# Small reciprocals before the broadcast, squares and text context on GpSimd, exponentials ahead of the stages, and a later context load in a cross-attention and mixture-of-experts kernel

## The reference

```python
x = x + xattn(layernorm(x), ctx)          # x: 8 x 112 x 512, ctx: 8 x 375 x 512, 16 heads of 32
x = x + moe(layernorm(x))                 # 8 experts, the best 2 of each token
# xattn: ctx_img = ctx[:, :257], ctx_txt = ctx[:, 257:]
q     = rms_norm(linear(x, q_w, q_b), norm_q_w)
k     = rms_norm(linear(ctx_txt, k_w, k_b), norm_k_w);          v     = linear(ctx_txt, v_w, v_b)
k_img = rms_norm(linear(ctx_img, k_img_w, k_img_b), norm_k_img_w); v_img = linear(ctx_img, v_img_w, v_img_b)
out   = linear(attention(q, k, v) + attention(q, k_img, v_img), o_w, o_b)
# rms_norm: y * rsqrt(mean(y*y) + eps), so every projection is squared and summed over its 512 channels
# attention: softmax(q k / sqrt(32)) v, so every head has two sums of exponentials, one over image and one over text keys
```

## Time and profile before

| | us |
|---|---|
| three runs: median (lowest to highest) | 931.02 (930.43 to 933.33) |
| the profiled execution | 931.23 |
| its span from first to last instruction | 929.4 |
| TensorE matmul busy | 773.7 (83%) |
| VectorE busy | 588.3 (63%) |
| ScalarE busy | 505.8 (54%) |
| GpSimd busy | 69.6 (7%) |
| reciprocals L761, 32 of them | 55.7, mean 1741 ns |

### The profile page before, as it was taken

One profiled execution on the slowest core, in us unless ns is written; L12 is line 12 of the kernel. 1 busy time (PEld: TensorE's weight loads), 2 busy tenths in 40 slices (PEclk: granted clock), 3 DMA queues, 4 the chain that ended last, 5 costly groups with the idle time before them and its releaser, 6 DMA issues.

```text
span 929.4 us, 17429 instructions
## 1 busy us (share of the span) xinstructions
PE 773.7 (83%) x6238; PEld 676.3 (73%) x6238; DVE 588.3 (63%) x1001; ACT 505.8 (54%) x1154; POOL 69.6 (7%) x94
## 2 busy tenths in 40 slices
PE   2888989898989898773079999999999999999930
PEld 2566666666666666552079999999999999999920
DVE  5466767676767676746136767676767676767634
ACT  4566767676767676751044545454545555555510
POOL 2100000000000000000600000000000000000014
PEclk9989999999999999855579999999999999999975
DMA  7850102010202000407625656565656565656568
GB/s 245 312 210 1 64 11 64 12 64 11 63 12 65 11 22 11 158 11 260 204 86 187 233 184 236 185 235 183 236 184 236 184 236 184 234 183 237 181 226 259
DMA packets 33982, 137.53 MB, mean 148 GB/s; under 512 B 3712, under 2 KB 3728, under 8 KB 22928
## 3 DMA queue, kind: packets, MB, share of 16 engines
q1 hardware_dynamic: 31200, 129.23, 40.0%
q0 software_dynamic: 2736, 7.69, 2.9%
HBM read 115.36 MB, written 21.54 MB: 147 GB/s over the span
## 4 chain that ended last, share of the span: by engine, by line
PE 68%; DVE 9%; ACT 9%; issue 7%; DMA 3%; POOL 2%; SPq 0%; POOLq 0%; ACTq 0%; DVEq 0%
PE tiles L960 7%; PE tiles L962 7%; PE tiles L961 7%; PE scores L1191 4%; PE scores L1193 4%; PE scores L1192 4%; PE ptb L1051 3%; PE pvb L962 3%; PE pvb L961 3%; PE pvb L960 3%; PE ptb L962 3%; PE ptb L961 3%; PE ptb L960 3%; PE scores L1042 2%; ACT scr L543 2%
## 5 line engine op out<-in xcount | busy, mean ns | idle before, releaser
L776 DVE TENSOR_TENSOR w<-scr,w 128x2048 fp32r<-128x2048 f32 x76 | 174.2, 2292 | 84.6 <-ACT w L568 84.6
L568 ACT ACTIVATE w<-scr 128x2048 fp32r<-128x2048 f32 x76 | 144.8, 1907 | 63.2 <-PE scores L1193 59.3
L960 PE MATMUL tiles<-c,w 128*128 128x256 f32 (+1 forms) x272 | 83.0, 305 | 22.1 <-DVE c L672 17.5
L1051 PE MATMUL ptb<-ident,scr 112*128 112x112 f32 x384 | 64.4, 279 | 25.9 <-ACT scr L553 25.9
L960 PE MATMUL tiles<-w 128*128 128x256 f32 x288 | 81.5, 283 | 0.0
L961 PE MATMUL tiles<-w 128*128 128x256 f32 x288 | 81.5, 283 | 0.0
L962 PE MATMUL tiles<-w 128*128 128x256 f32 x288 | 81.5, 283 | 0.0
L961 PE MATMUL tiles<-c,w 128*128 128x256 f32 (+1 forms) x272 | 79.9, 294 | 0.0
L962 PE MATMUL tiles<-c,w 128*128 128x256 f32 (+1 forms) x272 | 79.9, 294 | 0.0
L1051 PEld LDWEIGHTS ptb<-ident,scr 112*128 112x128 f32 x384 | 44.1, 149 | 48.9 <-ACT scr L545 35.1
L553 ACT ACTIVATE scr<-ptb 128x336 f32<-128x336 f32 x128 | 59.9, 468 | 26.9 <-PE ptb L1051 26.9
(11 more groups left out here) (212 smaller groups left out, 2120.9 us busy)
## 6 DMA issues: line engine op xcount, KB each, us to landing
scr<-in_dram SPq DMA_DIRECT2D x86, 1024.0 KB, 4.8
slots_d<-xr SPq DMA_DIRECT2D x3, 2048.0 KB, 17.5
scr<-in_dram SPq DMA_DIRECT2D x8, 750.0 KB, 4.9
scr<-slots_d SPq DMA_DIRECT2D x10, 512.0 KB, 4.6
slots_d<-scr SPq DMA_DIRECT2D x9, 512.0 KB, 3.8
xn<-in_dram SPq DMA_DIRECT2D x10, 256.0 KB, 4.7
xb<-in_dram SPq DMA_DIRECT2D x8, 224.0 KB, 4.9
xr<-in_dram SPq DMA_DIRECT2D x8, 224.0 KB, 2.5
```

Of the source, the lines that this page charges most:

```text
L568: act.activation(EH[slot], raw[slot], ACT.Copy).then_inc(S["eh_done"], 1)
L776: dve.tensor_tensor(EL[slot], raw[slot], EH[slot].bitcast(F32), ALU.subtract).then_inc(S["el_done"], 1)
L960: pe.matmul(out, wh, xh, start=start, stop=False)
L1051: mm = pe.transpose(ptb[:, t * L:(t + 1) * L], probs[0:L, h % 4, t * P:(t + 1) * P], ident[0:L, 0:L])
```

## The change

- `invert_sums`: the eight sums are inverted into a small tile `rsum` (112 x 8); VectorE waits for that on a semaphore `inverted`, and copies it 32 times into `rx`.
- The six squares of a body go from ScalarE to GpSimd (`square`, a product of `kn` or `qn` with itself), in the order k0, [second layer norm's power], k1, k2, q, kx, k3.
- The high part of the text context goes from ScalarE (h = 2) to GpSimd, between the first layer norm's power and k0's square; its low part on VectorE moves from h = 3 to h = 6. Image part and text part get semaphores of their own. In body -1 both stay as they were.
- ScalarE at h = 0, 4, 8, 12 runs `weigh` ahead of the stages.
- SP loads the next context behind the store of x1 (in body -1 behind the load of x).

```diff
+            def next_context(b):
+                sp.wait_ge(S["ch0_done"], b + 2)
+                sp.wait_ge(S["ch1_done"], b + 2)
+                sp.wait_ge(S["cl_done"], 2 * (b + 2))
+                sp.dma_start(cr, ctxT[b + 2]).then_inc(S["c_in"], 16)
...
                     if b < LAST - 1:
-                        sp.wait_ge(S["ch_done"], 2 * (b + 2))
-                        sp.wait_ge(S["cl_done"], 2 * (b + 2))
-                        sp.dma_start(cr, ctxT[b + 2]).then_inc(S["c_in"], 16)
                         sp.wait_ge(S["xn_done"], b + 2)
                         sp.dma_start(xb[0:L, :], x[b + 2]).then_inc(S["x_in"], 16)
+                    if b < FIRST:
+                        next_context(b)
...
                     sp.dma_start(x1_d[b - 1], x1[0:L, :]).then_inc(S["x1_stored"], 16)
+                if FIRST <= b < LAST - 1:
+                    next_context(b)
+                if has_tail(b):
...
+            def square(name, b, p):
+
+                taken(pool, name, b)
+                if name == "q":
+                    to, of = sq[:, :, 0:L], qn[:, 1 - p, :, :]
+                elif name == "kx":
+                    to, of = sq[:, :, L + IMG:TOK], kn[1 - p][:, :, IMG:KEYS]
+                else:
+                    c = int(name[1])
+                    to, of = sq[:, c, L:L + IMG], kn[1 - p][:, c, 0:IMG]
+                pool.tensor_tensor(to, of, of, ALU.mult).then_inc(S["squares"], 1)
+
             def body(b, p):
                 if has_prep(b):
                     rstd(b + 2, mv1, ve1, rs1, "ln1")
+                    if not fixed(b, -1):
+                        pool.wait_ge(S["c_in"], 16 * (b + 2))
+                        taken(pool, "v2", b)
+                        pool.tensor_copy(c_part(cH)[1], cr[:, :, PARTS[1]]).then_inc(S["ch1_done"], 1)
+                    if not fixed(b, -1):
+                        pool.wait_ge(tile_ready[tile_use("ms", b - 1)[0]], tile_use("ms", b - 1)[1] + 1)
+                    square("k0", b, p)
                 if has_tail(b):
                     rstd(b, mv2, ve2, rs2, "ln2")
                 if has_prep(b):
+                    for name in ("k1", "k2", "q", "kx", "k3"):
+                        square(name, b, p)
...
-                if name == "q":
-
-                    taken(act, "q", b)
-                    act.activation(sq[:, :, 0:L], qn[:, 1 - p, :, :], ACT.Square).then_inc(S["squares"], 1)
...
-                    act.activation(sq[:, c, L:L + IMG], tiles[:, bank, 0:IMG], ACT.Square, bias=bias).then_inc(S["squares"], 1)
...
-                if name == "kx":
-                    taken(act, "kx", b)
-                    act.activation(sq[:, :, L + IMG:TOK], kn[1 - p][:, :, IMG:KEYS], ACT.Square).then_inc(S["squares"], 1)
...
+                    if h % 4 == 0 and has_heads(b):
+                        weigh(b, p, h)
                     for name in STAGE_AT[h]:
                         if has(name, b):
                             stage(name, b, p)
-                    if h % 4 == 0 and has_heads(b):
-                        weigh(b, p, h)
-                    if h == 2 and has_prep(b) and not fixed(b, -1):
-                        split_ctx(act, b + 2, 1)
...
-                dve.reciprocal(rx[0:L], sums[0:L, g % 2, :, :].unsqueeze(3).to_broadcast([L, 2, 4, HD])).then_inc(S["rsum_done"], 1)
+                dve.reciprocal(rsum[0:L], sums[0:L, g % 2, :, :]).then_inc(S["inverted"], 1)
+                dve.wait_ge(S["inverted"], NC * b + g + 1)
+                dve.tensor_copy(rx[0:L], rsum[0:L].unsqueeze(3).to_broadcast([L, 2, 4, HD])).then_inc(S["rsum_done"], 1)
...
-                    if h in (1, 3) and has_prep(b) and not fixed(b, -1):
-                        split_ctx_low(b + 2, h // 2)
+                    if h in (1, 6) and has_prep(b) and not fixed(b, -1):
+                        split_ctx_low(b + 2, h // 5)
```

More of the change, by code:

```diff
@@ L135, in cross_attention_moe @@
         vx = sb("vx", [P, 2, D])
-        rx = sb("rx", [P, 2, 4, HD])
+        rsum, rx = sb("rsum", [P, 2, 4]), sb("rx", [P, 2, 4, HD])
         rbc, pvn, af = sb("rbc", [P, 2 * L]), sb("pvn", [P, 2 * L]), sb("af", [P, L])
@@ L238, in cross_attention_moe @@
             "vbias_done", "nq_done", "vlast_mm", "vlast_sb", "vlast_out",
-            "x_in", "c_in", "ch_done", "cl_done", "xr_in", "xr_ob", "ln1_stats", "ln1_mv", "ln1_var", "ln1_rstd", "xn_done",
+            "x_in", "c_in", "ch0_done", "ch1_done", "cl_done", "xr_in", "xr_ob", "ln1_stats", "ln1_mv", "ln1_var", "ln1_rstd", "xn_done",
             "ln2_stats", "ln2_mv", "ln2_var", "ln2_rstd", "xh_done",
             "squares", "sum_a", "sum_b", "r_done", "rms_done", "q_done", "k_done", "qh_done", "ql_done", "kh_done", "kl_done", "rows_stored", "rows_in",
-            "s_ready", "max_done", "exp_done", "rsum_done", "t_ready", "pt_done",
+            "s_ready", "max_done", "exp_done", "inverted", "rsum_done", "t_ready", "pt_done",
             "pv_ready", "rb_done", "pv_read", "a_done", "cleared", "ah_done", "al_done", "x1_stored",
@@ L279, in split_ctx @@
             act.wait_ge(S["c_in"], 16 * n)
-            act.activation(c_part(cH)[i], cr[:, :, PARTS[i]], ACT.Copy).then_inc(S["ch_done"], 1)
+            act.activation(c_part(cH)[i], cr[:, :, PARTS[i]], ACT.Copy).then_inc(S[("ch0_done", "ch1_done")[i]], 1)
         @block.sync
@@ L670, in split_ctx_low @@
             def split_ctx_low(n, i):
-                dve.wait_ge(S["ch_done"], 2 * n - 1 + i)
+                dve.wait_ge(S[("ch0_done", "ch1_done")[i]], n)
                 dve.tensor_tensor(c_part(cL)[i], cr[:, :, PARTS[i]], c_part(cH)[i].bitcast(F32), ALU.subtract).then_inc(S["cl_done"], 1)
```

## The result

The changed kernel takes 919.44 us in the median of four runs (918.5 to 922.8) against 931.18 for the kernel before (930.43 to 933.33): a ratio of 0.9877 with a 95% interval of 0.9846 to 0.9907, that is 11.7 us or 1.2% less. The forecast was 923.0, with a range from 916 to 932. The profiled execution took 922.8, the longest of its four; a second profile of the same kernel took 917.89.

A forecast was written before the change was run, and what follows sets the result against it. A body was taken as TensorE's work plus its short waits, mostly caused by ScalarE. Gains of 2.72 us against losses of 1.0 and 0.3 made -1.42 a steady body, -8.0 with the other bodies: 923.0 us, range 916 to 932.

The forecast's parts named there:

- (1): k0's wait for the image context's low part, behind VectorE's long reciprocal, ends with the small reciprocal and copy: 0.49 us gained.
- (2): The second scores' wait for head 3's exponential ends, as Square and context copy leave ScalarE: 0.78 us a body gained.
- (3): Head 4's transposes no longer wait for a ScalarE copy, with `weigh` run first: 0.49 us a body gained.
- (4): Head 8's transposes no longer wait, with `weigh` first and one k2 copy gone from ScalarE: 0.96 us gained.
- kx and k3 on GpSimd: At the fourth scores, these squares make VectorE's sums and maxima 1.35 us late; the body loses 1.0.
- collision at h = 3: GpSimd's context copy and k0's square meet VectorE's two-input L772; it slips in between them, losing 0.3 us a body.
- rival A: VectorE isn't held up by GpSimd: a steady body gains 2.27 us, 917 in all; chance 0.14.
- rival B: GpSimd wins at h = 3 and L772 waits for copy and square: -0.72 a body, 927.5 us; chance 0.12.
- if L833 starts while k3's square runs, the blocking is wrong: Sign at VectorE's sum: starting before GpSimd's k3 square ends would show VectorE isn't held, so A holds.
- Rival D: Slower: kx and k3 squares on GpSimd cost twice the price, 3.8 us the pair; 938 us, chance 0.12.
- since it asks first: At h = 3, VectorE's L772 slips in between GpSimd's copy and k0's square: 0.3 us lost, 1.0 if waiting for both.
- Rival C: ScalarE's exponentials come first but only wait for something else, so (3) and (4) stay: 932 us, chance 0.12.

The follow-up runs named there:

- the second experiment: The kernel before with only the exponentials put ahead of the stages at every fourth head: 923.63 us, ratio 0.9909.
- them and both edits: The changed kernel with k0's square later on GpSimd and the squares of kx and k3 back on ScalarE: 909.94 us, ratio 0.976.

## Why the prediction was right, and where its terms were off

**The four waits.** All four went. Their sizes by the stretches and the single edits:

| term | forecast | measured |
|---|---|---|
| (1) k0's wait, reciprocal | -0.49 | -0.71 (reciprocal alone) |
| (2) second scores | -0.78 | -0.70 (-1.41 of the first stretch, less (1)) |
| (3) transposes of head 4 | -0.49 | -0.52 (exponentials alone) |
| (4) transposes of head 8 | -0.96 | -1.03 (third stretch) |
| kx and k3 on GpSimd | +1.00 | +0.57 (fourth stretch; gone with both on ScalarE) |
| collision at h = 3 | +0.30 | +0.57 (gone with k0's square later) |
| a steady body | -1.42 | -1.87 (11.22 over six) |

The measured terms make -1.82. The rest lies in the second stretch: 9.81 with k0's square later, 9.88 with the exponentials first alone; which part of the change gives it, no run isolates. All four waits that were to go went, and both losses came. The sum was 0.45 a body too cautious, and six bodies make 2.7 of the 3.6 us between 923.0 and 919.4.

The time alone is weak evidence for this. 919.44 lies at the very edge of the forecast's own 919.5 to 926.5 and is nearer to rival A's 917 than to 923.0. It came so near in part by luck: the collision at h = 3 went the way of rival B (0.27 more than forecast), and the squares of kx and k3 hid that (0.43 less than forecast, mostly because they are shorter than priced). Only the rows and the single edits tell the forecast from A. (The range is said to begin at "A's 916"; A's own sum is 917.)

**Term (1), sized too small.** The profile's 0.49 counts from the modelled end of a matmul, and for (2) to (4) the prediction added 0.15 for that. For (1) it did not. In the changed kernel k0 starts 0.18 after the start of the two transposes ahead of it, and 0.89 before: a wait of 0.71 hidden behind a row of 0.48 or 0.49. The copy and the small reciprocal cost what was assumed, 0.52 from the start of the first to the end of the second:

```profile
143.13 0.20 DVE L780 RECIPROCAL rsum<-sums 112x8 f32<-112x8 f32 x1
143.36 0.29 DVE L782 COPY rx<-rsum 112x256 f32<-112x256 f32 x1
```

**Term (2)** is what the second scores win by two edits together. Undoing one of them gives back 0.34 (text context on ScalarE) or 0.19 (squares on ScalarE) in the first stretch.

**Term (4) needs both edits.** With the exponentials first alone the third stretch wins 0.68. The remaining 0.35 comes only with the squares off ScalarE, as the two kernels with them there (0.68, 0.68) and the two without (1.03, 1.06) show. TensorE's starts tell where it goes: with the squares on ScalarE kt's first matmul comes 0.2 later, and the transposes of head 8 come another 0.15 later behind kt's, both too short for a row of waits. Of this stretch's squares only k2's stands ahead of both in ScalarE's order; no run moves it by itself.

**The squares, priced too high.** Groups by line and form in the changed kernel:

```profile
L452 POOL TENSOR_TENSOR scr<-scr 128x257 f32<-128x257 f32 x32 | 20.0, 624 | 58.6 <-ACT scr L535 58.6
L452 POOL TENSOR_TENSOR scr<-scr 128x472 f32<-128x472 f32 x8 | 7.8, 973 | 43.2 <-DVE scr L757 43.2
L452 POOL TENSOR_TENSOR scr<-qn 128x448 f32<-128x448 f32 x8 | 7.5, 937 | 3.1 <-DVE qn L752 3.0
```

0.62, 0.97 and 0.94 instead of 0.73, 1.18 and 1.13; the pair kx and k3 takes 1.55 in a row, not 1.91. L448, from which the price was taken, reads two different tensors; a square reads the same one twice. Whether that is the cause, no run isolates.

**The chain at the fourth scores.** Body 2 of the changed kernel, against the earlier trace rows:

```profile
169.97 0.64 DVE L757 TENSOR_TENSOR scr<-tiles,vec 128x472 f32<-128x472 f32 x1
...
170.69 1.55 POOL L452 TENSOR_TENSOR scr<-scr 128x472 f32<-128x472 f32 x2 [5.62 <-DVE scr L757]
...
171.70 1.06 DVE L854 TENSOR_TENSOR scr<-scr 128x487 f32<-128x487 f32 x1 [1.09 <-POOL scr L452]
...
173.96 0.68 DVE L772 TENSOR_REDUCE nmax<-scores 112x2 f32<-112x514 f32 x1
```

L854 starts when kx's square is done and lasts 1.06 instead of 0.67: it ends 0.52 after GpSimd's last square (172.24). Here the prediction's own sign misleads: "if L833 starts while k3's square runs, the blocking is wrong". Its successor L854 does start, at 171.70, while that square runs. The recorded start does not show that its data flow; the length does, 1.06 against 0.67 beside ScalarE's squares (the run with kx and k3 on ScalarE). From kx's bias to the maxima it is 3.99 instead of 3.16, +0.83 where +1.35 was forecast; 0.36 of the difference is the shorter pair. TensorE's ms waits 0.3 and the body loses 0.57. Rival D needed 3.1 us for the pair and is out.

**VectorE waits for GpSimd.** This was the step that no row showed. Timeline of body 2 at h = 3, against the earlier trace rows:

```profile
149.21 0.58 POOL L460 CAST c<-scr 128x472 fp32r<-128x472 f32 x1
149.29 0.78 PE L1063 MATMUL scores<-kq 32*112 32x376 f32 x12
149.55 0.94 DVE L793 TENSOR_TENSOR a<-af,a 128x112 fp32r<-128x112 f32 x1 [1.19 <-ACT a L584]
149.75 0.62 POOL L452 TENSOR_TENSOR scr<-scr 128x257 f32<-128x257 f32 x1
...
150.42 0.53 DVE L701 TENSOR_SCALAR xn<-xb,mv,rs 112x512 f32<-112x512 f32 x1
```

L793 (L772 before) was 0.28 and is 0.93 to 0.95 in all six steady bodies. It starts while the context copy runs, and ends 0.12 after k0's square, which started later than it: asking first did not help it, the next GpSimd instruction went ahead. The step of the forecast that failed here is "since it asks first". Rival B had it right, but its price of 1.0 was too high: copy and square are each some 0.1 shorter than priced, L793 is 0.66 longer than before, and the body loses 0.57. Moving the square took L793 back to 0.36. So each engine is seen waiting for the other, and rival A (917) is out, though the shorter squares brought the time to within 3 us of it. The Trainium skill (SBUF — State Buffer, "Who interferes with whom") says that the one that issues first holds the shared ports for its whole instruction. The traces agree for single instructions (L854's 1.06 beside k3's square; L793's 0.44 behind k0's square and L440's 1.05 beside L691, both in body 2 of the run with the text context on ScalarE). For two GpSimd instructions in a row, the context copy and k0's square, they add that VectorE, waiting since the first, also waits for the second.

**Rival C** (the exponentials only wait for something else) fell with the second experiment: 1.2 us a body from the order alone.

**SP, right for the wrong reason.** The prediction gave SP's part 0 and held it for unrelated. The whole change agrees with 0, but undoing it costs 29.5 us. The step that failed is "nothing is won", though the number 0 came out, by luck: the store's slack was looked at with the low part at h = 3, while the change puts that wait of SP three steps later. That this is the cause, the run with the low part back at h = 3 and the old order shows: 44.40 a body, as with the new order (44.38). The list of what stands behind the wait was made for the new order only.

**Bodies -1 and 0.** Body -1: +1.0 forecast, +0.99 in the second profile (48.20 against 47.21), with full clock at its end in both. The mechanism is seen too: TensorE's wait for the sums goes from 0.68 to 1.63, and with kx and k3 squared by ScalarE the first scores came at 47.06. Body 0: -0.5 forecast, -2.0 and -2.6 measured. The profile of before had two stretches of half clock in body 0 and the second profile of after none, so part of this is the clock; how much, these profiles don't tell.

## What to carry to other kernels

When the bound engine's waits are short and many, the order on the engine that feeds it can be worth more than the work taken off it: here the exponentials first (1.2 us a body) against all squares moved (a loss of 0.5). In this kernel work moved to an idle GpSimd was free only where VectorE had no instruction with two SBUF inputs at that time and nobody waited for the result. The four early squares were worth having (43.42 with them and both edits, 44.05 with all squares on ScalarE), the two late ones and the early place of k0's were not, and putting these right made 909.9 of 919.4. A wait that is moved in one engine's program moves everything queued behind it: check each order against each other change, not only the whole.

## What the runs showed of the hardware that was not expected

- VectorE waiting for GpSimd's first instruction also waits for the next one, 0.93 to 0.95 instead of 0.28 (six bodies of the changed kernel, context copy and k0's square).
- A GpSimd instruction that only writes does not hold a two-input VectorE instruction (0.38 beside copy and memset, 0.37 beside the copy alone), but a TENSOR_SCALAR of 512 elements with its tensor in SBUF went from 0.53 to 0.69 and ended 0.28 after the memset. The Trainium skill (SBUF — State Buffer, "Who interferes with whom") says that such instructions can run in a mode with both port pairs and then exclude any GpSimd instruction; the two lengths agree with that.
- One element in a square on GpSimd costs 1.6 ns (from 624 ns for 257 to 973 for 472), against 2.1 for the sum of two tensors.
- TensorE's clock fell for 10.2 us at the end of body -1 in one execution of the changed kernel and stayed full there in another, 3.5 us apart. It also fell there in a profile of the kernel before with only SP's order changed (granted clock 0.83 from 37 to 47 us).
